# Two-layer graph network, between the layers: GpSimd waits for its own gathers every eight, VectorE scales x1 from the fourth block on

## The chip, the cores and the metric

The kernel runs on one core of a Trainium2 chip. The metric is the device time of the whole program in microseconds (us). Three executions of the kernel before gave 2437.67, 2437.79 and 2443.56 us, a median of 2437.79. A further execution was taken with the hardware profiler: 2439.11 us, of which 2437.4 us lie between the first and the last instruction (the span).

## The reference

There are 6250 nodes with 128 features and 100000 edges, sorted by their target node. Layer 0 computes a message for each edge, takes the maximum over the edges of each target, adds it to the node's features and normalizes each row. Layer 1 sums the weighted rows of the sources into each target, multiplies by a weight matrix, adds a bias and the residual, and normalizes again.

```python
h = x @ W1 + b1
e = concatenate([h[dst], h[src] - h[dst]], axis=-1)
m = relu(relu(e @ W2 + b2) @ W3 + b3)
x = layernorm(x + relu(segment_max(m, dst, num_segments=6250)))      # layer 0, then x1
AX = segment_sum(edge_weight[:, None] * x[src], dst)
x = layernorm(x + (AX @ W.T + b))                                    # layer 1
```

## The kernel before, in words

The nodes are held as 49 columns of 128 rows, one node per partition. The program has four stages: preparation of tables (to about 118 us of the span), the edge loop of layer 0 (to about 1360 us), the stretch between the layers (1360 to 1468 us), and layer 1 (the rest: a loop over 196 groups of edges, then a loop that sums 409 pairs of tiles). Each engine has an instruction list written out by hand; the order in it is the order of issue, and the lists meet only at semaphores. The change touches the stretch between the layers alone.

What each engine does there, with its lines in the kernel before:

- GpSimd (POOL) gathers the maxima. The edge loop left running maxima in the table `seg_tab` in memory; for each of the 49 node columns one indirect DMA (line 455) brings the 128 rows at the ends of the nodes' segments into `rows`. The 49 columns form seven blocks of 8, 8, 8, 8, 8, 6 and 3 columns (`NORM`, semaphores `seg_ld`, each with its own). The dictionary `beats` lets GpSimd wait before columns 24, 28, 32, 36, 40, 44 and 46 until VectorE has reached a given block.
- VectorE (DVE), after it has built small tables and one-hot matrices (line 929), adds the gathered rows to `x` for a block (line 1173), takes the moments (lines 1109 and 1112), and after ScalarE's square root makes the reciprocal and the shift (lines 1119 and 1120, semaphore `rstd_done`).
- ScalarE (ACT) takes the square root of a block (line 729), scales and shifts it into `x1` (line 735, one instruction for each column, semaphore `x1_done`), and copies finished products to their compact places (`place`, line 673). A place copy goes to an offset that is read from memory into registers first (line 666), and each of the 49 copies waits for the one before. Places of a block follow two blocks behind its scaling (`BEHIND = 2`).
- TensorE (PE) compacts: for each batch of four columns it multiplies `x1` by the one-hot matrices (line 1377), into one of four PSUM banks. When all 49 columns are placed it multiplies the compact nodes by the layer's weights (line 1521, 13 batches, `xw`). ScalarE copies the even batches out of PSUM (line 746), VectorE the odd ones (line 1225).
- SyncE (SP) issues 50 stores of zeros of 200 KB each (line 562) into the table of layer 1, behind them four loads of `row_bc` (line 516) that VectorE needs for its first `pick` matrices (line 1187), then four more, then the stores of `xw` (line 577) and the loads of layer 1's windows of rows (line 572). They stand in one list, so that none can overtake the zeros.

In VectorE's list the four first picks and four small tables (line 1194) stand ahead of its first copy of `xw`. They wait for all blocks of `x1` and for SyncE's loads of `row_bc`.

Of the kernel before, what the change touches and what calls it, by code (L numbers as in the profile page):

```python
# [12 lines left out]
GT = 4  # L13
# [5 lines left out]
G = T // GT  # L19
UN = 4  # L20
IT = G // UN
RING = 3 * UN
RB = 6
AHEAD = 4
LATE = 2
BEHIND = 2
BEAT = 5
# [6 lines left out]
NORM = [8, 8, 8, 8, 8, 6, 3]  # L34
NC = len(NORM)
# [30 lines left out]
NB = -(-H // GT)  # L66
# [7 lines left out]
ALU = mybir.AluOpType  # L74
# [8 lines left out]
def gnn_kernel(nc, x, src, dst, edge_weight, W1, b1, W2, b2, W3, b3, WL, bL, out):  # L83
    ds = bass.ds
    IOA = bass.IndirectOffsetOnAxis
    with ExitStack() as ctx:
# [6 lines left out]
        def sem(name):  # L93
            return ctx.enter_context(nc.semaphore(name))

        def dram(name, shape, dt=F32):
# [59 lines left out]
        chunk_of = [c for c in range(NC) for _ in range(NORM[c])]  # L156
# [175 lines left out]
        x1_sum, var_done, std_done, rstd_done, x1_done = map(  # L332
            sem, ("x1_sum", "var_done", "std_done", "rstd_done", "x1_done"))
        res_done = sem("res_done")
        rel_ready, perm_step, perm_ready, vals_ps, vals_in = map(sem, ("rel_ready", "perm_step", "perm_ready", "vals_ps", "vals_in"))
# [39 lines left out]
        def batch(b):  # L375

            return range(b * GT, min(H, (b + 1) * GT))
# [7 lines left out]
        def _(pool):  # L385
# [64 lines left out]
            pool.wait_ge(vals_ps, G)  # L450
            beats = {24: (rstd_done, 2), 28: (x1_sum, 3), 32: (rstd_done, 3), 36: (x1_sum, 4), 40: (rstd_done, 4), 44: (x1_sum, 5), 46: (rstd_done, 5)}
            for h in range(H):
                if h in beats:
                    pool.wait_ge(*beats[h])
                pool.indirect_dma_start(rows[:, h, :], None, seg_tab[:, :],
                                        IOA(ap=end_i[:, h:h + 1], axis=0)).then_inc(seg_ld[chunk_of[h]], 16)

# [171 lines left out]
        def _(act):  # L629
# [100 lines left out]

            for c, cols in enumerate(norm_cols):
                roots(0, c)
                act.wait_ge(rstd_done, c + 1)
                for h in range(cols.start, cols.stop):
                    last = nc.scalar.activation(x1[:, h, :], x1_sums[:, h, :], ACT.Identity, bias=shift_by[:, h:h + 1], scale=rstd[:, h:h + 1])
                last.then_inc(x1_done, 1)
                for b in range(NB):
                    if chunk_of[batch(b)[-1]] + BEHIND == c:
                        place(1, b)
            for b in range(NB):  # L740
                if chunk_of[batch(b)[-1]] + BEHIND >= NC:
                    place(1, b)

# [65 lines left out]
        def _(dve):  # L809
# [305 lines left out]
            def scales(n, c):  # L1115

                cols = norm_cols[c]
                dve.wait_ge(std_done, n * NC + c + 1)
                link(V.reciprocal(rstd[:, cols], std[:, cols]))
                V.scalar_tensor_tensor(shift_by[:, cols], mv[:, cols, 0], -1.0, rstd[:, cols], ALU.mult, ALU.mult).then_inc(rstd_done, 1)  # L1120
# [49 lines left out]
            for c, cols in enumerate(norm_cols):  # L1170
                dve.wait_ge(seg_ld[c], 16 * NORM[c])
                for h in range(cols.start, cols.stop):
                    last = V.scalar_tensor_tensor(x1_sums[:, h, :], rows[:, h, :], full[:, h:h + 1], x_sb[:, h, :], ALU.mult, ALU.add)
                last.then_inc(x1_sum, 1)
                dve.wait_ge(x1_sum, c + 1)
                moments(c, x1_sums[:, cols, :])
                scales(0, c)


# [35 lines left out]

            dve.wait_ge(x1_done, NC)
            for r in range(UN):
# [70 lines left out]
        def _(pe):  # L1288
# [223 lines left out]
            for b in range(NB):  # L1512
                pe.wait_ge(x1_done, chunk_of[batch(b)[-1]] + 1)
                place(1, b)
# [86 lines left out]
```

## Time and profile before

| | us |
|---|---|
| median of three runs | 2437.79 |
| profiled execution | 2439.11 |
| its span | 2437.4 |
| TensorE busy | 1886.7 (77% of the span) |
| VectorE busy | 1538.1 (63%) |
| GpSimd busy | 1274.0 (52%) |
| ScalarE busy | 1004.5 (41%) |

The span divides into the stages above. In the page's picture of 40 slices TensorE shows 7 tenths through layer 0, a dip to 2 and 4 tenths in the two slices from 1341 to 1462 us, and 9 tenths through layer 1's loop. The stretch that the change touches lies in that dip. A row of a timeline gives the start, the duration, the engine, the line, the operation, the number of instructions merged into the row, and in brackets the idle time before it with what ended it.

### The profile page before, as it was taken

What the parts mean: (1) busy time and instruction counts of PE and PEld (TensorE: products, weight loads), DVE (VectorE), ACT (ScalarE), POOL (GpSimd) and SP (SyncE); (2) the same over time, 40 slices, a digit from 0 to 9 for tenths busy, and PEclk for the clock granted to TensorE, in tenths of its full rate; (3) what the DMA queues carried; (4) which work ended last, traced back from release to release, by engine and by line L of the source; (5) the groups of instructions that cost most, each with busy time, mean ns of one, the idle gap of its engine ahead of it and who ended that gap; (6) DMA issues with size and microseconds to landing.
All of it is one profiled execution on the core that took longest, in us unless ns stands there. A gap on an engine that the chain in (4) does not pass through costs nothing.

```text
span 2437.4 us, 59448 instructions
## 1 busy us (share of the span) xinstructions
PE 1886.7 (77%) x15384; PEld 1643.7 (67%) x15384; DVE 1538.1 (63%) x4339; ACT 1004.5 (41%) x3045; POOL 1274.0 (52%) x1300
## 2 busy tenths in 40 slices
PE   5657777777777777777777349989999999699994
PEld 5645555555555555555555248888888888699994
DVE  5556666666676766666666844544444444388886
ACT  3413233333233333323333155555555555466666
POOL 6366566666666666666665344666666666400000
PEclk8779899999999999999999669999999999899997
DMA  4445555555555555555555257777777777699995
GB/s 131 123 123 147 148 152 151 152 155 154 154 151 153 155 152 152 151 150 149 146 149 146 89 191 223 231 240 233 238 241 234 239 239 240 214 282 291 286 290 174
DMA packets 533245, 452.12 MB, mean 185 GB/s; under 512 B 59035, under 2 KB 498295, under 8 KB 533152
## 3 DMA queue, kind: packets, MB, share of 16 engines
q1 hardware_dynamic: 374544, 260.16, 37.2%
q0 software_dynamic: 53312, 138.17, 18.3%
q10 hardware_dynamic: 105296, 52.84, 7.4%
q14 instruction: 70, 0.57, 0.1%
q8 instruction: 23, 0.38, 0.1%
HBM read 291.57 MB, written 159.37 MB: 185 GB/s over the span
## 4 chain that ended last, share of the span: by engine, by line
PE 40%; DVE 21%; issue 14%; another core or an unknown queue 14%; DVEq 3%; DMA 3%; ACT 3%; SPq 1%; POOL 0%; ACTq 0%; POOLq 0%
PE z_ps L1542 8%; PE t_ps L1542 7%; PE m_ps L1542 7%; DVE run L1058 7%; DVE whole L1036 4%; DVE oh L957 2%; PE z_ps L1568 2%; PE m_ps L1568 2%; PE z_ps L1467 2%; DMA whole<-tab 2%; PE t_ps L1568 2%; PE t_ps L1476 2%; PE m_ps L1454 2%; PE m_ps L1455 1%
## 5 line engine op out<-in xcount | busy, mean ns | idle before, releaser
L445 POOL DMA_INDIRECT whole<-q_tab,src_ti x784 | 763.0, 973 | 484.9 <-remote 259.8
L468 POOL DMA_INDIRECT tab<-whole,row_at x392 | 405.9, 1036 | 271.9 <-issue 83.2
L1187 DVE TENSOR_SCALAR whole<-row_bc,node_id 128x768 f32<-128x768 uint8 x392 | 229.4, 627 | 332.3 <-DMA row_bc<-rel_tab 281.5
L690 ACT ACTIVATE m<-m_ps,bias 128x512 f32<-128x512 f32 x196 | 134.7, 687 | 677.7 <-remote 641.7
L1454 PE MATMUL m_ps<-ident,whole 128*128 128x128 f32 x1568 | 322.3, 288 | 34.4 <-issue 21.3
L1455 PE MATMUL m_ps<-oh,win 128*128 128x128 f32 x1568 | 314.6, 284 | 1.3 <-issue 1.3
L1454 PEld LDWEIGHTS m_ps<-ident,whole 128*128 128x128 f32 x1568 | 257.0, 205 | 70.4 <-issue 69.8
L985 DVE TENSOR_TENSOR scratch<-s_ps,blk_oh 128x196 f32<-128x196 f32 x196 | 70.6, 360 | 318.5 <-remote 314.2
L1455 PEld LDWEIGHTS m_ps<-oh,win 128*128 128x128 f32 x1568 | 250.9, 201 | 1.9 <-issue 1.9
L1058 DVE TENSOR_TENSOR_SCAN run<-row_bc,run,z_ps 128x512 f32<-128x512 uint8 x195 | 248.2, 1273 | 0.4 <-ACT z_ps L695 0.3
L1476 PEld LDWEIGHTS t_ps<-ident,run 128*128 128x128 f32 x784 | 111.4, 153 | 188.2 <-issue 177.6
L1467 PE MATMUL z_ps<-m,w 128*128 128x512 f32 x392 | 234.7, 683 | 0.0
L1249 DVE TENSOR_TENSOR whole<-iota_f,whole 128x256 f32<-128x256 f32 (+1 forms) x409 | 184.4, 451 | 60.4 <-PE z_ps L1568 32.1
L1476 PE MATMUL t_ps<-ident,run 128*128 128x128 f32 x784 | 157.8, 297 | 71.9 <-issue 69.1
L1542 PE MATMUL t_ps<-win,whole 128*128 128x128 f32 x1560 | 194.6, 279 | 18.9 <-issue 14.5
L1542 PE MATMUL z_ps<-win,whole 128*128 128x128 f32 x1584 | 197.3, 279 | 12.3 <-issue 11.8
L1414 PE MATMUL s_ps<-whole 128*128 128x18 bf16 x784 | 48.4, 171 | 201.0 <-issue 166.2
L1542 PE MATMUL m_ps<-win,whole 128*128 128x128 f32 x1560 | 194.2, 279 | 11.7 <-issue 11.3
L1542 PEld LDWEIGHTS t_ps<-win,whole 128*128 128x128 f32 x1560 | 181.1, 192 | 19.6 <-issue 15.3
L1542 PEld LDWEIGHTS z_ps<-win,whole 128*128 128x128 f32 x1584 | 183.5, 192 | 13.8 <-issue 13.1
L1414 PEld LDWEIGHTS s_ps<-whole 128*128 128x128 bf16 x784 | 36.4, 96 | 230.5 <-issue 228.9
L1542 PEld LDWEIGHTS m_ps<-win,whole 128*128 128x128 f32 x1560 | 180.7, 192 | 13.6 <-issue 13.0
(294 smaller groups left out, 3592.3 us busy)
## 6 DMA issues: line engine op xcount, KB each, us to landing
whole<-tab SPq DMA_DIRECT2D x409, 194.0 KB
win<-p_tab SPq DMA_DIRECT2D x784, 64.0 KB
seg_tab<-run_e ACTq DMA_DIRECT2D x196, 256.0 KB
win<-xw_tab SPq DMA_DIRECT2D x392, 128.0 KB
row_bc<-seg_row_tab SPq DMA_DIRECT2D x196, 128.0 KB
row_bc<-rel_tab SPq DMA_DIRECT2D x196, 96.0 KB
tab<-zeros SPq DMA_DIRECT2D x67, 200.0 KB
whole<-q_tab,src_ti POOLq DMA_INDIRECT x784
```

Of the source, the lines that this page charges most:

```text
L445: pool.indirect_dma_start(qg[:, g % RING, j, :], None, q_tab[:, :], IOA(ap=src_ti[:, t:t + 1], axis=0)).then_inc(q_ld[g % RING], 16)
L468: pool.indirect_dma_start(tab[:, :], IOA(ap=row_at[0:FR, k:k + 1], axis=0), fat[0:FR, k % RR, :], None).then_inc(fat_st[k // GK % RS], 16)
L690: nc.scalar.activation(m1[:, s, :], m1_ps[:, s, :], ACT.Relu, bias=bias12[:]).then_inc(relu1, 1)
L1058: V.tensor_tensor_scan(run[:, s, :], row_bc[:, r % RB, GE:2 * GE], z_ps[:, s, :], first, ALU.mult, ALU.max).then_inc(run_done, 1)
L1187: last = V.tensor_scalar(pick[:, s, j, :], row_bc[:, s, 0:GK * SLOTS], node_id[:, j:j + 1], None, ALU.is_equal)
L1249: V.tensor_tensor(node_hot[:, r % PS, 0:n, :], iota_f[:, :].unsqueeze(1).to_broadcast([P, n, P]), loaded[:, r % PL, 0:n * KW].rearrange("p ...
L1454: mm(m1_ps[:, s, c], lhsT=qg[:, r % RING, j, :], rhs=ident[:], start=True, stop=False)
L1455: last = mm(m1_ps[:, s, c], lhsT=win[:, r % UN, j, :], rhs=oh[:, s, c], start=False, stop=True)
L1467: mm(z_ps[:, s, :], lhsT=w3[:], rhs=m1[:, s, :], start=True, stop=True).then_inc(z_done, 1)
L1476: last = nc.tensor.transpose(t_ps[:, s, c], run[:, s, c], ident[:])
L1542: last = mm(fat_bank[r % 3][0:FR, c, q * P:(q + 1) * P], lhsT=pick[:, r % UN, j, (c * SL + q) * FR:(c * SL + q + 1) * FR], rhs=win[:, r % ...
L1568: last = mm(sum_bank[r % PS], lhsT=node_hot[:, r % PS, q, :], rhs=loaded[:, r % PL, q * KW:q * KW + D], start=q == 0, stop=q == SL - 1)
```

## The change

Four things are changed.

1. GpSimd's `beats` go. In their place it waits before columns 8, 16, 24, 32, 40 and 46 until the gather of the column two before (6, 14, 22, 30, 38, 44) has landed. These six gathers count on semaphores of their own (reused ones of the edge loop); VectorE waits for them beside its block's.
2. In blocks 3 to 6 (25 columns) VectorE makes `x1` itself with one `tensor_scalar` for each column, right behind the block's scales. Blocks 0 to 2 stay with ScalarE.
3. ScalarE's list is written in another order: three blocks scaled, then the places of block 0, the root of block 3, the places of block 1, the root of block 4, the places of blocks 2 and 3, the root of block 5, the places of block 4, the root of block 6, the places of blocks 5 and 6.
4. TensorE and VectorE wait for `x1_done` (blocks 0 to 2) or `x1_late` (blocks 3 to 6).

```diff
-BEHIND = 2
+EARLY = 3
+RESTS = [8, 16, 24, 32, 40, 46]
+FLY = 2
...
+        rest_ld = dict(zip([h - FLY for h in RESTS], q_ld))
+        landed = {h: 16 * (GT * len(range(k, G, RING)) + 1) for k, h in enumerate(rest_ld)}
...
-            beats = {24: (rstd_done, 2), 28: (x1_sum, 3), 32: (rstd_done, 3), 36: (x1_sum, 4), 40: (rstd_done, 4), 44: (x1_sum, 5), 46: (rstd_done, 5)}
             for h in range(H):
-                if h in beats:
-                    pool.wait_ge(*beats[h])
+                if h in RESTS:
+                    pool.wait_ge(rest_ld[h - FLY], landed[h - FLY])
                 pool.indirect_dma_start(rows[:, h, :], None, seg_tab[:, :],
...
-            for c, cols in enumerate(norm_cols):
+            for c, cols in enumerate(norm_cols[:EARLY]):
                 roots(0, c)
                 act.wait_ge(rstd_done, c + 1)
                 for h in range(cols.start, cols.stop):
                     last = nc.scalar.activation(x1[:, h, :], x1_sums[:, h, :], ACT.Identity, bias=shift_by[:, h:h + 1], scale=rstd[:, h:h + 1])
                 last.then_inc(x1_done, 1)
...
+            places_of(0)
+            roots(0, 3)
+            places_of(1)
+            roots(0, 4)
+            places_of(2)
+            places_of(3)
+            roots(0, 5)
+            places_of(4)
+            roots(0, 6)
+            places_of(5)
+            places_of(6)
...
                 scales(0, c)
+                if c >= EARLY:
+                    dve.wait_ge(rstd_done, c + 1)
+                    for h in range(cols.start, cols.stop):
+                        last = V.tensor_scalar(x1[:, h, :], x1_sums[:, h, :], rstd[:, h:h + 1], shift_by[:, h:h + 1], ALU.mult, ALU.add)
+                    last.then_inc(x1_late, 1)
...
-            dve.wait_ge(x1_done, NC)
+            dve.wait_ge(x1_done, EARLY)
+            dve.wait_ge(x1_late, NC - EARLY)
```

ScalarE's list before, from the last place copy of block 0 over block 3's root and scaling to block 1's first places:

```order
L673 ACTIVATE whole<-m_ps 128x128
L729 ACTIVATE std<-mv,eps 128x8
L735 ACTIVATE whole<-whole,shift_by,rstd 128x128 x8
L666 TENSOR_LOAD col_off_i
L673 ISA
L673 ACTIVATE whole<-z_ps 128x128
```

The same place in ScalarE's list of the changed kernel (its line numbers are its own):

```order
L677 ACTIVATE whole<-m_ps 128x128
L733 ACTIVATE std<-mv,eps 128x8
L670 TENSOR_LOAD col_off_i
L677 ISA
L677 ACTIVATE whole<-z_ps 128x128
```

The eight scaling instructions of the block are gone from between the root and the places.

VectorE's list before, from block 3's sums to block 4's (`whole` holds `rows`, `x1_sums` and `x1`):

```order
L1173 SCALAR_TENSOR_TENSOR whole<-whole,full 128x128 x8
L1109 BN_STATS part<-whole 128x6 x8
L1112 BN_AGGR mv<-part 128x2 x8
L1119 RECIPROCAL rstd<-std 128x8
L1120 SCALAR_TENSOR_TENSOR shift_by<-mv,rstd 128x8
L1173 SCALAR_TENSOR_TENSOR whole<-whole,full 128x128 x8
```

The same place in the changed kernel:

```order
L1190 SCALAR_TENSOR_TENSOR whole<-whole,full 128x128 x8
L1123 BN_STATS part<-whole 128x6 x8
L1126 BN_AGGR mv<-part 128x2 x8
L1133 RECIPROCAL rstd<-std 128x8
L1134 SCALAR_TENSOR_TENSOR shift_by<-mv,rstd 128x8
L1198 TENSOR_SCALAR whole<-whole,rstd,shift_by 128x128 x8
L1190 SCALAR_TENSOR_TENSOR whole<-whole,full 128x128 x8
```

The scaling now stands on VectorE between a block's scales and the next block's sums. GpSimd's and SyncE's lists hold the same DMAs in the same order; only GpSimd's waits differ.

## Rows read from the trace of the kernel before

**Rows 1.** GpSimd's timeline: start, duration, engine, line, operation, count, idle before

```profile
1372.80 1.45 POOL L455 DMA_INDIRECT whole<-seg_tab,end_i  x1 [0.30 <-issue]
...
1391.67 0.94 POOL L455 DMA_INDIRECT whole<-seg_tab,end_i  x1 [0.30 <-issue]
1401.76 1.07 POOL L455 DMA_INDIRECT whole<-seg_tab,end_i  x1 [9.14 <-DVE shift_by L1120]
...
1410.68 0.94 POOL L455 DMA_INDIRECT whole<-seg_tab,end_i  x1 [0.30 <-issue]
...
1420.72 0.94 POOL L455 DMA_INDIRECT whole<-seg_tab,end_i  x1 [0.30 <-issue]
1425.57 1.07 POOL L455 DMA_INDIRECT whole<-seg_tab,end_i  x1 [3.91 <-DVE shift_by L1120]
...
1436.01 1.11 POOL L455 DMA_INDIRECT whole<-seg_tab,end_i  x1 [0.30 <-issue]
```

**Rows 2.** SyncE's timeline, 1384 to 1466 us, the zeros by stretch

```profile
1384.31 9.73 SPq L562 DMA_DIRECT2D tab<-zeros  x5
1395.45 8.65 SPq L562 DMA_DIRECT2D tab<-zeros  x12
1403.81 17.20 SPq L562 DMA_DIRECT2D tab<-zeros  x9
1423.81 6.81 SPq L562 DMA_DIRECT2D tab<-zeros  x8
1431.38 4.35 SPq L562 DMA_DIRECT2D tab<-zeros  x3
1437.86 9.85 SPq L562 DMA_DIRECT2D tab<-zeros  x14
1447.76 8.22 SPq L516 DMA_DIRECT2D row_bc<-rel_tab  x8
...
1465.15 0.99 SPq L572 DMA_DIRECT2D win<-xw_tab  x2
```

**Rows 3.** VectorE's timeline, 1360 to 1458 us

```profile
1360.51 3.22 DVE L929 TENSOR_SCALAR win<-iota_f,in_col 128x128 f32<-128x128 f32 x16
...
1373.36 0.77 DVE L1149 CAST whole<-slot_vals 128x1176 int32<-128x1176 f32 x1
...
1386.37 1.64 DVE L1109 BATCH_NORM_STATS2 part<-whole 128x6 f32<-128x128 f32 x8
1392.66 0.88 DVE L1112 BATCH_NORM_AGGREGATE mv<-part 128x2 f32<-128x6 f32 x8 [4.65 <-remote]
...
1413.66 2.19 DVE L1173 SCALAR_TENSOR_TENSOR whole<-whole,full 128x128 f32<-128x128 f32 x8 [6.95 <-DMA whole<-seg_tab,end_i]
...
1417.56 0.64 DVE L1112 BATCH_NORM_AGGREGATE mv<-part 128x2 f32<-128x6 f32 x8
...
1451.31 4.32 DVE L1187 TENSOR_SCALAR whole<-row_bc,node_id 128x768 f32<-128x768 uint8 x8 [5.57 <-DMA row_bc<-rel_tab]
1455.55 1.42 DVE L1194 TENSOR_TENSOR junk<-iota_f,whole 114x256 bf16<-114x256 f32 x4
1457.78 0.69 DVE L1225 COPY whole<-m_ps 128x512 f32<-128x512 f32 x1 [0.81 <-PE m_ps L1521]
```

**Rows 4.** ScalarE's timeline, 1395 to 1454 us

```profile
1395.52 0.30 ACT L729 ACTIVATE std<-mv,eps 128x8 f32<-128x8 f32 x1 [35.75 <-remote]
...
1406.75 3.18 ACT L735 ACTIVATE whole<-whole,shift_by,rstd 128x128 f32<-128x128 f32 x8 [0.47 <-issue]
...
1424.56 0.30 ACT L729 ACTIVATE std<-mv,eps 128x8 f32<-128x8 f32 x1 [11.33 <-remote]
...
1453.88 0.28 ACT L673 ACTIVATE whole<-m_ps 128x128 f32 x1 [0.22 <-ACT whole L673]
```

**Rows 5.** TensorE's timeline: first product of line 1521, first of layer 1's loop

```profile
1454.21 3.53 PE L1521 MATMUL m_ps<-wT,whole 128*128 128x128 f32 x16 [4.62 <-ACT whole L673]
...
1468.42 2.92 PE L1542 MATMUL z_ps<-win,whole 128*128 128x128 f32 x24
```

More of the change, by code:

```diff
@@ L333, in gnn_kernel @@
             sem, ("x1_sum", "var_done", "std_done", "rstd_done", "x1_done"))
+        x1_late = sem("x1_late")
+        rest_ld = dict(zip([h - FLY for h in RESTS], q_ld))
+        landed = {h: 16 * (GT * len(range(k, G, RING)) + 1) for k, h in enumerate(rest_ld)}
         res_done = sem("res_done")
@@ L450, in _ @@
             pool.wait_ge(vals_ps, G)
-            beats = {24: (rstd_done, 2), 28: (x1_sum, 3), 32: (rstd_done, 3), 36: (x1_sum, 4), 40: (rstd_done, 4), 44: (x1_sum, 5), 46: (rstd_done, 5)}
             for h in range(H):
-                if h in beats:
-                    pool.wait_ge(*beats[h])
+                if h in RESTS:
+                    pool.wait_ge(rest_ld[h - FLY], landed[h - FLY])
                 pool.indirect_dma_start(rows[:, h, :], None, seg_tab[:, :],
-                                        IOA(ap=end_i[:, h:h + 1], axis=0)).then_inc(seg_ld[chunk_of[h]], 16)
+                                        IOA(ap=end_i[:, h:h + 1], axis=0)).then_inc(rest_ld.get(h, seg_ld[chunk_of[h]]), 16)
             pool.wait_ge(fat_zero, 1)
@@ L729, in roots, with places_of @@
                 nc.scalar.activation(std[:, cols], mv[:, cols, 1], ACT.Sqrt, bias=eps[:]).then_inc(std_done, 1)
-            for c, cols in enumerate(norm_cols):
+            def places_of(c):
+                for b in range(NB):
+                    if chunk_of[batch(b)[-1]] == c:
+                        place(1, b)
+            for c, cols in enumerate(norm_cols[:EARLY]):
                 roots(0, c)
@@ L736, in _ @@
                 last.then_inc(x1_done, 1)
[L737 to L742, printed above, removed]
+            places_of(0)
[9 more added lines that the diff above has]
+            places_of(6)
             for b in range(0, HX // GT, 2):
@@ L1170, in _ @@
             for c, cols in enumerate(norm_cols):
-                dve.wait_ge(seg_ld[c], 16 * NORM[c])
+                dve.wait_ge(seg_ld[c], 16 * (NORM[c] - sum(h in rest_ld for h in range(cols.start, cols.stop))))
+                for h in range(cols.start, cols.stop):
+                    if h in rest_ld:
+                        dve.wait_ge(rest_ld[h], landed[h])
                 for h in range(cols.start, cols.stop):
@@ L1177, in _ @@
                 scales(0, c)
+                if c >= EARLY:
+                    dve.wait_ge(rstd_done, c + 1)
+                    for h in range(cols.start, cols.stop):
+                        last = V.tensor_scalar(x1[:, h, :], x1_sums[:, h, :], rstd[:, h:h + 1], shift_by[:, h:h + 1], ALU.mult, ALU.add)
+                    last.then_inc(x1_late, 1)
             def picks(i, r):
@@ L1512, in _ @@
             for b in range(NB):
-                pe.wait_ge(x1_done, chunk_of[batch(b)[-1]] + 1)
+                c = chunk_of[batch(b)[-1]]
+                if c < EARLY:
+                    pe.wait_ge(x1_done, c + 1)
+                else:
+                    pe.wait_ge(x1_late, c - EARLY + 1)
                 place(1, b)
```

## The prediction

> **What bounds the kernel now.** I read the profile in this order: the page (span 2437.4 us, where TensorE dips), then the timelines of the five engines through the stretch between the layers, and last SyncE's list in short windows. The question is which wait ends last before layer 1's loop starts at 1468.42 [rows 5]. Behind that point TensorE's lists of layer 1 are untouched, so a microsecond at the start is taken as a microsecond at the end.
>
> Two chains meet there. The first is the chain of x1: gathers, sums, moments, root, scale, place. Its last place copy starts at 1453.88 and ends at 1454.16 [rows 4], and TensorE starts the products of line 1521 at 1454.21 [rows 5]. It is long because of two pauses of GpSimd, 9.14 and 3.91 us, both ended by VectorE's scales [rows 1], and two late starts that no instruction explains: VectorE's aggregates at 1392.66 after 4.65 us idle, and ScalarE's root at 1424.56, although the aggregates it waits for started at 1417.56 and took 0.64, so 6.36 us late [rows 3, 4].
>
> The second is SyncE's list. Its 50 zero stores end at 1447.71, the first row_bc load is issued at 1447.76 [rows 2], and VectorE's picks, which need it, start at 1451.31 after 5.57 us of waiting for that DMA [rows 3]. Picks and tables keep VectorE until 1456.97 (1455.55 + 1.42), and only then can it copy an odd batch of xw; it does so at 1457.78 [rows 3]. So the two chains arrive 0.81 us apart. An earlier x1 gives at most little until SyncE's list is earlier too.
>
> The reader is to see one thing more in rows 1 and 2 together. SyncE issues zeros fast when GpSimd pauses and slowly when it gathers: 12 in 8.65 us and 14 in 9.85 (0.70 to 0.72 each), against 9 in 17.20 (1.91 each) and 5 in 9.73 (1.95) while gathers run. The gain is not instant: after GpSimd restarts at 1401.76 SyncE stays fast for about 2 us, after 1425.57 for about 5, and after GpSimd stops at 1392.61 it resumes at 1395.45. The two unexplained late starts lie in the slow stretches too: VectorE resumes at 1392.66, just when GpSimd's 24th gather ends, and ScalarE at 1395.52 and at 1424.56, each 2.9 us after GpSimd stopped (1392.61, 1421.66).
>
> **The change part by part.**
>
> GpSimd's waits. Two pauses of 9.14 and 3.91 us go (13.05, against 0.30 between any two gathers, so 12.45 us above the ordinary gap). Six rests come. The price of one: a gather lands about 2.0 us after its issue ends (the last of block 3 ended at 1411.62, VectorE starts at 1413.66 [rows 1, 3]). The gather before a rest ends 1.25 us after the one waited for, so the rest is 2.0 - 1.25 = 0.75, with 0.2 for the semaphore 0.95, which is 0.65 above the ordinary gap. Bounds: nothing (already landed) to about 2 us (landing slowed by the zeros). Six make 3.9 us. The last gather starts at 1436.01 - 12.45 + 3.9 = 1427.5 and lands at about 1430.5 instead of 1439. Queued behind a rest is only the next gather.
>
> Scaling on VectorE. 25 instructions of 128x128, which the trace does not show. The nearest rows: 3.22 us for 16 tensor_scalars of line 929 (0.20 each) below, 2.19 for 8 of line 1173 (0.27 each) above [rows 3]. I take 0.20, since it is the same operation and shape: 8 cost 1.6 us, all 25 cost 5.0 (at most 6.8). They stand between blocks, where VectorE waited 6.95 us for a gather in block 3 [rows 3]; gathers come 10 us a block and VectorE needs 2.2 + 1.6 + 0.6 + 0.7 + 0.4 + 1.6 = 7.1, so gathers cover it. On ScalarE 25 scalings of 0.40 (3.18 for 8 [rows 4]) go, 10 us.
>
> The new end of the x1 chain, if no start is late: block 6 is summed from 1430.5, VectorE needs 0.9 + 0.7 + 0.3 + 0.7 + 0.4 + 0.6 = 3.6 us for three columns, TensorE and ScalarE then take two batches, some 4 us: 1438. Against 1454.16 that is 16 us earlier. With the 4.65 and 6.36 us of late starts put back it is 1449, still 5 earlier. So this chain stops being the last.
>
> What is late next: SyncE. Its 50 zeros take 63.4 us from 1384.31. Slow stretches hold 5 + 9 + 3 = 17 (one zero is counted in two windows, so 16) in about 36.6 us, 2.3 each with the gaps between; the other 34 take 26 us, 0.7 to 0.75 each [rows 2]. In the changed kernel gathers run from 1361 to 1428.5, so the slow state would last from 1384.3 to about 1429.5, 45 us instead of 36.6: 45 / 2.3 = 19.6 zeros, and 30.4 at 0.70 = 21.3 us, an end at 1450.8, 3.1 later than before. Each of the four rests that fall after 1384 gives some fast time back. If a rest gave 3 us as the two restarts did, 12 us fast hold 16 zeros, 33 us slow hold 14.3, and 19.7 are left for 13.8 us: an end at 1443.3, 4.4 earlier. A rest is shorter than those pauses and one gather is still in flight, so I take half: 1447, 0.7 earlier. Both ends stay in the range.
>
> What an early x1 gives by itself. With places done by 1449 TensorE fills its four banks and one more, and waits for VectorE's first odd copy, now at 1457.0 instead of 1457.78. It has then eight batches left. From a cold clock the first two cost 3.53 for 16 products and the other six 0.9 each [rows 5]: 1457.7 + 3.5 + 5.4 = 1466.6, where the last product before ended at 1467.57. That is 1.0 us. SyncE's window loads at 1465.15 [rows 2] come 1 to 2 us earlier the same way, since its stores find batches ready.
>
> Sum, against the profiled execution: 2439.1 - 0.7 (SyncE) - 1.0 (products) = 2437.4. The profiled execution lies 1.3 us above the median of the runs shown, so the median to expect is 2436.
>
> One rule speaks against the change. The trace first: gathers beside the tensor_scalars of line 929 took 0.94 to 1.04 us, and one beside the casts of 1176 elements took 1.45 [rows 1, 3], 0.5 more. The Trainium skill ("SBUF — State Buffer", section "SBUF: two separate sides") says that VectorE in a mode with two ports locks GpSimd out, so that it cannot write descriptors, for the whole instruction. By the rule the 25 scalings of 0.20 would hold up gathers by up to 5 us; by the row of line 929 they hold up none. The x1 chain has the room either way.
>
> **The rivals.**
>
> A. The rests do all that the long pauses did: no late starts and SyncE mostly fast. For it: SyncE's restart graces are long, and in layer 0's loop GpSimd rests briefly after every four gathers and all engines run. Against it: the late starts ended only with pauses of 9 and 4 us. All 50 zeros at 0.70 would end at 1419, so the x1 chain with its end at 1438 decides, and layer 1 starts up to 16 us earlier: 2423. Half of that, SyncE's end near 1440, gives 2439.1 - 8 - 1 = 2430, or 2429 as a median.
>
> B. Starved engines, slower. VectorE's wait at 1388 and ScalarE's behind it were ended by GpSimd's pause at 1392.61. If a rest of 0.95 us with one gather in flight does not end such a wait, and it lasts until GpSimd is done at 1428.5, then VectorE and ScalarE take blocks 0 to 2 from 1431 on, 5.2 us a block, so to 1446.5, and ScalarE's 49 place copies, 1.67 us a batch of four, follow: 1467. Layer 1 starts 13 us late: 2452. It decides from the point where the late starts sum to over 16 us. A milder form is SyncE's end at 1450.8 alone: 3.1 - 1.0 = 2.1 us slower, 2440.
>
> C. The order does not matter: late starts are tied to something else, and the end is as before, 2438.
>
> **How the numbers follow.** Forecast (within 4 us of 2436, C and the mild form of B with it) 0.62; A 0.21; B in its strong form 0.17. This kernel's measurement tells a change from none at about 0.3%, 7.3 us. A reaches beyond that in nearly all of its weight, B as well: faster 0.20, same 0.63, slower 0.17. The forecast's own range is 2431 to 2441. The range reaches to half of A and half of B: 2427 to 2447.
>
> **What would show it.** Right: GpSimd's gathers of line 459 in the changed kernel end near 1428.5 with six gaps of about 1 us; places end before 1450; VectorE's picks still wait for row_bc, at 1448 to 1454; the first product of layer 1's loop starts at 1465 to 1470. The scaling shows about 0.20 us an instruction. Wrong to the fast side: zeros at 0.7 us through the gathers and picks before 1445. Wrong to the slow side: a gap of over 10 us on VectorE or ScalarE between 1388 and 1430 that ends with GpSimd's last gather. Wrong altogether: a difference that lies outside the stretch, in either loop.

## The result, and the profile after

The changed kernel takes 2449.74 us (median of nine runs, 2447.59 to 2456.72), the kernel before 2438.89 (nine runs beside them, 2436.62 to 2443.56). The ratio is 1.0051, with a 95% interval of 1.0041 to 1.0062: slower, by 10.9 us between the medians, and outside the predicted range of 2427 to 2447. The profiled execution of the changed kernel took 2447.59 us with a span of 2445.9, so it is 8.5 us longer than that of before. It divides like this: the first gather of the stretch starts 1.1 us later (1362.37 against 1361.28), the stretch from there to the first product of layer 1's loop is 5.3 us longer (112.4 against 107.1), and the rest 2.1 us (971.1 against 969.0). The change has its work in the middle part only.

GpSimd's gathers in the changed kernel, to be set beside [rows 1]; the first, the six behind the rests, and the last:

```profile
1362.37 0.94 POOL L459 DMA_INDIRECT whole<-seg_tab,end_i  x1 [23.90 <-DMA seg_tab<-run_e]
...
1373.03 1.00 POOL L459 DMA_INDIRECT whole<-seg_tab,end_i  x1 [0.54 <-DMA whole<-seg_tab,end_i]
...
1385.13 3.04 POOL L459 DMA_INDIRECT whole<-seg_tab,end_i  x1 [0.83 <-DMA whole<-seg_tab,end_i]
...
1398.10 0.94 POOL L459 DMA_INDIRECT whole<-seg_tab,end_i  x1 [1.19 <-DMA whole<-seg_tab,end_i]
...
1408.92 0.94 POOL L459 DMA_INDIRECT whole<-seg_tab,end_i  x1 [0.69 <-DMA whole<-seg_tab,end_i]
...
1419.12 0.94 POOL L459 DMA_INDIRECT whole<-seg_tab,end_i  x1 [0.47 <-DMA whole<-seg_tab,end_i]
...
1427.05 0.94 POOL L459 DMA_INDIRECT whole<-seg_tab,end_i  x1 [0.74 <-DMA whole<-seg_tab,end_i]
...
1429.54 0.94 POOL L459 DMA_INDIRECT whole<-seg_tab,end_i  x1 [0.30 <-issue]
```

GpSimd does what it should, but for one gather of 3.04 us behind the second rest. The rests are 0.47 to 1.19 us, and the last gather ends at 1430.5 instead of 1437.1. VectorE behind it, to be set beside [rows 3]:

```profile
1409.92 2.19 DVE L1190 SCALAR_TENSOR_TENSOR whole<-whole,full 128x128 f32<-128x128 f32 x8 [3.52 <-DMA whole<-seg_tab,end_i]
1413.56 1.64 DVE L1123 BATCH_NORM_STATS2 part<-whole 128x6 f32<-128x128 f32 x8 [1.45 <-DVE whole L1190]
1424.08 0.58 DVE L1126 BATCH_NORM_AGGREGATE mv<-part 128x2 f32<-128x6 f32 x7 [8.88 <-issue]
1425.45 0.18 DVE L1126 BATCH_NORM_AGGREGATE mv<-part 128x2 f32<-128x6 f32 x1 [0.80 <-issue]
1434.22 0.20 DVE L1133 RECIPROCAL rstd<-std 128x8 f32<-128x8 f32 x1 [8.58 <-ACT std L733]
...
1434.66 2.14 DVE L1198 TENSOR_SCALAR whole<-whole,rstd,shift_by 128x128 f32<-128x128 f32 x8
...
1454.10 0.86 DVE L1198 TENSOR_SCALAR whole<-whole,rstd,shift_by 128x128 f32<-128x128 f32 x3
1455.05 4.32 DVE L1209 TENSOR_SCALAR whole<-row_bc,node_id 128x768 f32<-128x768 uint8 x8
1459.29 1.42 DVE L1216 TENSOR_TENSOR junk<-iota_f,whole 114x256 bf16<-114x256 f32 x4
1463.03 0.69 DVE L1248 COPY whole<-m_ps 128x512 f32<-128x512 f32 x1 [2.31 <-PE m_ps L1548]
```

And ScalarE, beside [rows 4]:

```profile
1405.67 0.30 ACT L733 ACTIVATE std<-mv,eps 128x8 f32<-128x8 f32 x1 [6.72 <-remote]
...
1433.88 0.30 ACT L733 ACTIVATE std<-mv,eps 128x8 f32<-128x8 f32 x1 [20.32 <-remote]
...
1458.88 0.28 ACT L677 ACTIVATE whole<-m_ps 128x128 f32 x1 [0.22 <-ACT whole L677]
```

The reader is to see a hole in block 3. VectorE has the data of the block at 1409.92, and ScalarE takes its root at 1433.88, 24 us later; what lies between is 4.6 us of work on VectorE. The statistics start 1.45 us after the sums. The aggregates wait 8.88 us behind their own engine's statistics, and the page says "issue", which means that it sees nothing they waited for. ScalarE then starts 8.3 us after the last of them ended (1425.63), at 1433.88, which is 3.4 us after GpSimd's last gather. Two rests of GpSimd lie in the hole (1419.12 and 1427.05) and end neither wait. VectorE's wait does end while GpSimd still gathers, ScalarE's only after the last gather. So of the lateness 11.1 us (1.45 + 8.88 + 0.80) lie on VectorE with gathers still coming, and 8.3 on ScalarE. From 1434 on VectorE works through blocks 4 to 6 without any such gap (the longest, 1.79 us, is behind place copies in ScalarE's list), but all gathers had been issued by 1430.5, and the picks of line 1209 start at 1455.05 with no wait for row_bc: VectorE itself is now the last.

SyncE's zeros, by stretch, beside [rows 2] (one zero stands in both of the last two stretches):

```profile
1385.33 8.91 SPq L566 DMA_DIRECT2D tab<-zeros  x11
1395.51 7.62 SPq L566 DMA_DIRECT2D tab<-zeros  x7
1404.22 18.42 SPq L566 DMA_DIRECT2D tab<-zeros  x7
...
1433.15 5.18 SPq L566 DMA_DIRECT2D tab<-zeros  x5
1438.00 11.72 SPq L566 DMA_DIRECT2D tab<-zeros  x19
...
1449.77 9.95 SPq L520 DMA_DIRECT2D row_bc<-rel_tab  x8
```

SyncE issues 18 zeros by 1403.1 (0.99 us each) while gathers run, then 9 in the 28.9 us up to 1433.15 (3.2 each), and the last 23 in 16.6 (0.72 each).

TensorE, beside [rows 5], and the granted clock of its first 4 us and of the rest of line 1548 (the columns of the second view: stretch, length, busy time and count of TensorE, its weight loads, VectorE, ScalarE and GpSimd, granted clock, DMA share, GB/s):

```profile
1459.20 3.78 PE L1548 MATMUL m_ps<-wT,whole 128*128 128x128 f32 x16 [1.70 <-ACT whole L677]
...
1474.80 2.92 PE L1569 MATMUL z_ps<-win,whole 128*128 128x128 f32 x24
```

```profile
1459.00:1463.00 4.00, 3.79 (x18) 3.80 (x19) 1.71 (x5) 0.75 (x2) 0.00 (x0) 0.50 0.22 68
1463.00:1474.80 11.80, 11.07 (x91) 10.90 (x90) 4.43 (x9) 3.58 (x6) 0.00 (x0) 0.91 0.66 183
```

The same two stretches of the kernel before:

```profile
1454.00:1458.00 4.00, 3.79 (x20) 3.79 (x21) 3.19 (x9) 0.76 (x2) 0.00 (x0) 0.58 0.34 93
1458.00:1468.40 10.40, 9.67 (x88) 9.51 (x87) 4.21 (x9) 3.58 (x6) 0.00 (x0) 1.00 0.74 205
```

The places end at 1458.88 + 0.28 = 1459.16, 5.0 us later than before, and from TensorE's first product of the layer's weights to layer 1's loop it takes 15.6 us instead of 14.2, since the granted clock is 0.50 and 0.91 there instead of 0.58 and 1.00 (0.50 is TensorE's lower level of 1.2 GHz, 1.00 its upper one of 2.4). Ahead of both stretches the engine had only short bursts of work with idle time between them. In three of the kernels below, with other waits, the same products took 14.3, 15.0 and 15.4 us (the first, the third and the second kernel of the first set).

One number serves in all that follows. From the first sum of a block of eight (line 1190) to ScalarE's root it takes 4.57 us where nothing is late. What goes beyond it is called the lateness of a block. In the kernel before it is 6.8 us in block 0 and 6.3 in block 3; in the changed kernel 2.1 in block 2 and 19.4 in block 3 (1433.88 - 1409.92 - 4.57).

### The profile page after: what moved, and what is told of

It is laid out like the page before. It is cut to its first block and busy times, and to the rows that moved or that the text cites. A ratio compares the mean times of both kernels' runs of the same rounds, so it can differ in the third digit from the quotient of the medians.

```text
span 2445.9 us, 59454 instructions
## 1 busy us (share of the span) xinstructions
PE 1900.9 (78%) x15384; PEld 1657.7 (68%) x15384; DVE 1544.3 (63%) x4364; ACT 998.7 (41%) x3020; POOL 1278.4 (52%) x1300
## 5 line engine op out<-in xcount | busy, mean ns | idle before, releaser
L1477 PE MATMUL m_ps<-ident,whole 128*128 128x128 f32 x1568 | 327.9, 293 | 33.3 <-issue 21.2
L1499 PE MATMUL t_ps<-ident,run 128*128 128x128 f32 x784 | 156.8, 299 | 72.4 <-issue 68.0
L1569 PEld LDWEIGHTS z_ps<-win,whole 128*128 128x128 f32 x1584 | 183.7, 192 | 15.2 <-issue 14.6
```

The costliest lines, as they stand in the source:

```text
L1477: mm(m1_ps[:, s, c], lhsT=qg[:, r % RING, j, :], rhs=ident[:], start=True, stop=False)
L1499: last = nc.tensor.transpose(t_ps[:, s, c], run[:, s, c], ident[:])
L1569: last = mm(fat_bank[r % 3][0:FR, c, q * P:(q + 1) * P], lhsT=pick[:, r % UN, j, (c * SL + q) * FR:(c * SL + q + 1) * FR], rhs=win[:, r % ...
```

## The experiments

The kernels were run in five sets, each beside the kernel before on one chip. The first set met a chip like that of the result (the kernel before takes 2436.24 us there). The other four met chips on which the same kernel takes 2145 to 2150 us. Which chip a set would meet was not known when its expectations were written; those of the second set reckon with the first kind alone. The experiments are told by kernel, and the set is named. "Kind of chip" is only a name for these two speeds: each chip of the five sets was met in one of them only, so it isn't shown that the chip makes the difference and not the hour or what else ran.

**Half the change each (first set).** The first kernel keeps the scaling on VectorE and the new order, and takes the old waits of GpSimd back:

```diff
-        rest_ld = dict(zip([h - FLY for h in RESTS], q_ld))
+        rest_ld = {}
...
+            beats = {24: (rstd_done, 2), 28: (x1_sum, 3), 32: (rstd_done, 3), 36: (x1_sum, 4), 40: (rstd_done, 4), 44: (x1_sum, 5), 46: (rstd_done, 5)}
             for h in range(H):
-                if h in RESTS:
-                    pool.wait_ge(rest_ld[h - FLY], landed[h - FLY])
+                if h in beats:
+                    pool.wait_ge(*beats[h])
```

> The changed kernel with GpSimd's waits of before put back: the scaling on VectorE and ScalarE's new order stay. Theory S (the short rests leave GpSimd's stream unbroken and starve ScalarE and VectorE until it ends; the scaling is harmless): the late starts are back to 4 to 6 us, the places end by 1450, the time is 2434 to 2440, 9 to 15 us below the changed kernel. Theory V (the loss comes from the scaling on VectorE and the order of ScalarE's list): it stays near 2449.

2433.49 us, ratio 0.9990 (0.9982 to 0.9999). GpSimd's pauses are 5.75 and 2.94 us, the lateness is 2.0, 2.1 and 4.4 us in blocks 0, 1 and 3, and layer 1's loop starts at 1461.87:

```profile
1420.82 0.30 ACT L734 ACTIVATE std<-mv,eps 128x8 f32<-128x8 f32 x1 [10.06 <-remote]
...
1447.56 3.63 PE L1549 MATMUL m_ps<-wT,whole 128*128 128x128 f32 x16 [1.70 <-ACT whole L678]
```

The second is the kernel before (`x1` on ScalarE, its order) with the six short rests:

```diff
+RESTS = [8, 16, 24, 32, 40, 46]
+FLY = 2
...
-                if h in beats:
-                    pool.wait_ge(*beats[h])
+                if h in RESTS:
+                    pool.wait_ge(rest_ld[h - FLY], landed[h - FLY])
...
```

> The kernel before with GpSimd's six short rests in place of its seven beats, all else as before. Theory S: as slow as the changed kernel or slower, 2447 to 2456, with ScalarE's root of block 3 starting only 2 to 4 us after GpSimd's last gather. Theory V: 2430 to 2438, since the gathers end 7 us earlier.

2447.08 us, 1.0047 (1.0032 to 1.0061). Lateness 10.0 us in block 2 and 15.2 in block 3; in block 3 it is VectorE that stands, twice. The first of these waits ends while GpSimd gathers, the second 4.1 us after its last gather (which ended at 1430.04):

```profile
1413.61 0.30 ACT L732 ACTIVATE std<-mv,eps 128x8 f32<-128x8 f32 x1 [14.44 <-remote]
...
1427.70 1.71 DVE L1112 BATCH_NORM_STATS2 part<-whole 128x6 f32<-128x128 f32 x8 [9.50 <-remote]
1434.18 0.64 DVE L1115 BATCH_NORM_AGGREGATE mv<-part 128x2 f32<-128x6 f32 x8 [4.78 <-remote]
```

So the whole loss comes with the short rests; the scaling on VectorE, with ScalarE's new order, costs nothing and gives a little (0.1%, hardly clear of the noise).

**One landing more at each rest (first set).** The changed kernel, waiting for the gather just before the rest instead of the one before that:

```diff
-FLY = 2
+FLY = 1
```

> The changed kernel with each rest lasting until the gather just before it has landed, not the last but one. Rests of 2.2 us in place of about 0.8, the gathers end about 8 us later. Theory S, in the form that a drained gather queue ends a late start: no engine is late by more than 10 us, 2436 to 2444. In the form that only a long pause helps: 2449 to 2456. Theory V: 2449.

2432.88 us, 0.9985 (0.9976 to 0.9994): faster than the kernel before, by 3.4 us between the medians. The rests grow to 1.86 to 3.01 us, the last gather starts at 1436.76, and block 3 has no lateness at all (1416.33 - 1411.76 is 4.57):

```profile
1411.76 2.19 DVE L1190 SCALAR_TENSOR_TENSOR whole<-whole,full 128x128 f32<-128x128 f32 x8 [6.35 <-issue]
...
1416.33 0.30 ACT L733 ACTIVATE std<-mv,eps 128x8 f32<-128x8 f32 x1 [4.42 <-DVE mv L1126]
...
1424.73 1.00 POOL L459 DMA_INDIRECT whole<-seg_tab,end_i  x1 [3.01 <-DMA whole<-seg_tab,end_i]
...
1448.91 3.78 PE L1548 MATMUL m_ps<-wT,whole 128*128 128x128 f32 x16 [1.70 <-ACT whole L677]
```

A further 1.05 to 2.5 us of waiting at each of six places took away the 19.4 us of lateness in block 3. What stays is 1.7 us in block 1.

**The zeros out of the way (first set).** The changed kernel with all gathers held back until the zero stores have landed (the six short rests stay):

```diff
             pool.wait_ge(vals_ps, G)
+            pool.wait_ge(zero_st, 16 * (NPAIR - NF + NX))
             for h in range(H):
```

> The changed kernel with GpSimd's gathers held until SyncE's 50 zero stores have landed. The stores should take 0.7 us each with no gather beside them, so 1384 to 1420; the gathers run 1420 to 1485 alone, and the time is 2495 to 2510. If the late starts need the zero stores beside the gathers, none is over 2 us here; if the unbroken stream of gathers alone makes them, ScalarE or VectorE is again late by 5 to 20 us within it.

2508.12 us, 1.0285 (1.0270 to 1.0300), as it must be with the two one behind the other. What it was run for are the starts:

```profile
1385.49 34.48 SPq L567 DMA_DIRECT2D tab<-zeros  x50
...
1444.41 2.19 DVE L1191 SCALAR_TENSOR_TENSOR whole<-whole,full 128x128 f32<-128x128 f32 x8 [5.01 <-DMA whole<-seg_tab,end_i]
...
1453.31 0.57 DVE L1127 BATCH_NORM_AGGREGATE mv<-part 128x2 f32<-128x6 f32 x7 [5.04 <-issue]
1454.68 0.18 DVE L1127 BATCH_NORM_AGGREGATE mv<-part 128x2 f32<-128x6 f32 x1 [0.79 <-issue]
...
1464.51 0.30 ACT L734 ACTIVATE std<-mv,eps 128x8 f32<-128x8 f32 x1 [21.90 <-remote]
```

The gathers run without zeros from 1422.81 to 1485.5, and the lateness is 15.5 us in block 1 and 20.6 in block 2. The zeros aren't needed for it: on this kind of chip GpSimd's stream of gathers is enough. VectorE is undisturbed until 1448.3, when 20 gathers have been issued. Both waits of block 1 end while the gathers run, as the rows show (aggregates at 1453.31, root at 1464.51). The zeros alone take 0.69 us each, as against 1.29 beside the gathers in the changed kernel (64.39 / 50).

**The changed kernel again (third set, another chip).** No edit.

> The changed kernel once more, beside its variants and the kernel before on one chip. Where the kernel before takes about 2437 us (starved chip): 2446 to 2452, 0.4 to 0.6% slower than before, late starts over 10 us. Where it takes about 2146 us (a chip on which no start was late in four variants): 0.2 to 0.4% faster than before, 2138 to 2142, as the run without any wait was.

2147.27 us against 2149.12, 0.9991 (0.9981 to 1.0000). The rests are there (0.58, 0.81, 1.67, 1.58, 1.21 and 2.50 us), but no block has more than 0.03 us of lateness:

```profile
1166.34 39.17 SPq L566 DMA_DIRECT2D tab<-zeros  x50
...
1196.34 0.30 ACT L733 ACTIVATE std<-mv,eps 128x8 f32<-128x8 f32 x1 [3.47 <-DVE mv L1126]
...
1197.12 2.14 DVE L1198 TENSOR_SCALAR whole<-whole,rstd,shift_by 128x128 f32<-128x128 f32 x8
...
1197.32 0.96 POOL L459 DMA_INDIRECT whole<-seg_tab,end_i  x1 [0.30 <-issue]
1198.58 0.98 POOL L459 DMA_INDIRECT whole<-seg_tab,end_i  x1 [0.30 <-issue]
```

So the loss goes with the late starts, which are absent here, and the same instructions without them are no loss. The late starts aren't a matter of this stretch alone. These are the longest waits in layer 0's edge loop, in the kernel before on the first kind of chip (engine, line, what it waited for: us in total, times, longest):

```profile
ACT m L690 <- remote: 614.5, 178, 4.4
DVE scratch L985 <- remote: 294.7, 178, 2.1
POOL whole L445 <- remote: 250.8, 179, 2.4
```

and in the changed kernel, whose loop is the same, on the second kind (on the first kind its list is like that of before: ScalarE's wait is 593.2 us over 173 times, put down to "remote"):

```profile
ACT m L694 <- PE m_ps L1478: 406.4, 179, 5.7
...
PE m_ps L1477 <- DMA whole<-q_tab,src_ti: 151.5, 146, 2.7
```

On the first kind nearly every group of edges has a wait that the profile puts down to nothing on the core ("remote"); on the second kind there is none in the list. These waits stand there although GpSimd rests some 1.4 us after every four gathers of that loop, so short rests don't keep them away there either. How much of each is late start and how much ordinary waiting the list doesn't say. Of the 303 us between the two executions 219 lie ahead of the first gather, 15 in the stretch and 69 in layer 1.

**A probe (third and fourth sets).** The changed kernel with 60 VectorE instructions of one element a partition between the statistics and the aggregates of block 3, where the changed kernel stood for 8.88 us. If something like a supply of instructions is short, a gap should fall between them.

```diff
+                if c == 3 and probe:
+                    for k in range(60):
+                        V.memset(idle[:, k:k + 1], 0.0)
                 link(last)
...
-                moments(c, x1_sums[:, cols, :])
+                moments(c, x1_sums[:, cols, :], True)
```

> The changed kernel with 60 memsets of one element each, without any semaphore wait among them, in VectorE's list between block 3's statistics and the aggregates that wait for them. If the late starts are slow semaphores alone, the 60 follow each other in under 6 us even while the stream of gathers starves the others, and the gap comes after them; if VectorE is short of instructions, the 60 are themselves spread over 10 us or more, in bursts. Where nothing is starved: 60 in under 6 us and no gap.

> The changed kernel with 60 one-element memsets without waits between block 3's statistics and the aggregates on VectorE. Where other engines are starved (before at about 2437): under 6 us for the 60 and the gap behind them if slow semaphores make the late starts; 10 us or more, in bursts, if VectorE is short of instructions. At about 2146: 60 in under 6 us, no gap.

2151.23 and 2149.72 us, one run each, both on the second kind of chip. In the third set's:

```profile
1196.76 1.06 DVE L1127 MEMSET idle<- 128x1 f32 x59
```

No gap, and none to be found where nothing is late. It tells nothing apart.

**No rests (second, third and fourth sets).** The changed kernel without any wait between the gathers:

```diff
-RESTS = [8, 16, 24, 32, 40, 46]
+RESTS = []
...
-        rest_ld = dict(zip([h - FLY for h in RESTS], q_ld))
+        rest_ld = {}
```

> The changed kernel without any wait of GpSimd between its 49 gathers. The changed kernel's rests were 0.47 to 1.19 us. If they do nothing (a wait has to drain the gathers, theory D), this is within 3 us of the changed kernel, 2446 to 2453, with the late starts up to GpSimd's end near 1426. If they give some relief (what counts is the mean pace of the gathers, theory R), the starts are later still, and the time is 2452 to 2462.

> The changed kernel without any wait between the gathers, again. At about 2437 us for the kernel before: theory D (only a drained queue helps) within 3 us of the changed kernel; theory R (mean pace counts) 3 to 12 us slower than it. At about 2146: within 3 us of the changed kernel.

> The changed kernel without any wait between the gathers. At about 2437 us for the kernel before: theory D (only a drained queue helps) 2446 to 2453, within 3 us of the changed kernel there; theory R (mean pace counts) 2452 to 2462. At about 2146: 0.2 to 0.3% faster than before, as twice already.

2139.50 against 2146.22 (0.9973, 0.9960 to 0.9986), 2144.96 against 2149.12 (0.9980, 0.9968 to 0.9991) and 2142.00 against 2145.26 (0.9986, 0.9973 to 0.9998). The late starts that were expected aren't there. With them gone the kernel without waits is a little faster than the kernel before, three times over; against the changed kernel in the third set (0.9991) the intervals overlap. How such a kernel fares on the first kind of chip wasn't measured.

**A slower stream without rests (second to fifth sets).** As above, with a small GpSimd memset behind each gather that it waits for:

```diff
...
+                nc.gpsimd.memset(idle[:], 0.0).then_inc(pace, 1)
+                pool.wait_ge(pace, h + 1)
```

> As the run without waits, with one GpSimd memset of 128x128 on a spare tile behind each gather, waited for, which spreads the gathers to about 1.5 us each; the queue never drains before the end. Theory R (the others fall behind where GpSimd gathers faster than about one in 1.5 us): no start later than 4 us, gathers end near 1436, 2430 to 2440. Theory D: ScalarE and VectorE are late by 10 us or more from the 20th gather on, 2450 to 2460.

> The changed kernel without waits but with a GpSimd memset of 128x128 behind each gather, again. At about 2437 for the kernel before: theory R 2430 to 2440 and no start over 4 us late; theory D 2450 or more, with starts over 10 us late. At about 2146: 2144 to 2150, as before (2146.8).

> The changed kernel without waits but with a GpSimd memset of 128x128 behind each gather. At about 2437 for the kernel before: theory R 2430 to 2440 and no start over 4 us late; theory D 2450 or more with starts over 10 us late. At about 2146: the same as before.

> The changed kernel without waits but with a GpSimd memset of 128x128 behind each gather. At about 2437 for the kernel before: theory R (mean pace counts) 2430 to 2440 and no start over 4 us late; theory D (only a drained queue helps) 2450 or more with starts over 10 us late. At about 2146: the same as before, as twice already.

1.0009 (0.9995 to 1.0023), 0.9999 (0.9988 to 1.0010), 1.0010 (0.9996 to 1.0024) and 1.0002 (0.9990 to 1.0014). It was meant to tell whether the mean pace of the gathers or a drained queue decides. On chips without late starts it can't. The gathers there take 72.8 us from the first to the last start, instead of 64.2 without the memsets, and the gain of the kernel without rests is gone.

**Few full drains (second set).** The changed kernel with three rests, each waiting for the gather just before it:

```diff
-RESTS = [8, 16, 24, 32, 40, 46]
-FLY = 2
+RESTS = [16, 32, 46]
+FLY = 1
```

> The changed kernel with three rests (before columns 16, 32, 46) that last until the gather just before has landed. The first late start of all traces so far came no sooner than 20 gathers into an unbroken stream. Theory D: 16 gathers between drained queues make none over 3 us, the gathers end near 1432, 2428 to 2434. Theory R (mean 1.39 us a gather against 1.50 with six full drains and 1.31 in the changed kernel): late starts of 3 to 10 us, 2436 to 2445.

2143.33 us, 0.9986 (0.9972 to 1.0000), with rests of 1.79, 3.28 and 3.57 us. Again no lateness.

**Full drains with x1 on ScalarE (second and fourth sets).** The kernel before with six such rests. The edit is that of the second kernel of the first set, with this in place of its `FLY = 2`:

```diff
+FLY = 1
```

> The kernel before with six rests that last until the gather just before has landed, in place of its beats; the scaling of x1 stays on ScalarE in its old order. If the scaling on VectorE is worth something once the starts are in time, this is slower than the changed kernel with the same rests (2432.9), by up to 10 us: 2436 to 2443. If ScalarE's scaling was covered by the gathers, it is within 3 us, 2430 to 2436.

> The kernel before with six rests that drain the gathers, x1 scaled by ScalarE as before. At about 2437 for the kernel before: if the scaling on VectorE is worth something once the starts are in time, 3 to 10 us slower than the changed kernel with the same rests (2432.9), so 2436 to 2443; if not, 2430 to 2436. At about 2146 it was 2154.9.

2154.93 us (1.0044, 1.0029 to 1.0060) and 2152.44 us (1.0032, 1.0021 to 1.0043): slower. The last place copy starts 89.4 us after the first gather (1237.99 - 1148.63), in the changed kernel of the third set 81.5 (1225.17 - 1143.68). Of these 7.9 us 3.3 come from the gathers, which take longer with full drains (74.0 us from the first to the last start against 70.7). Behind the last gather's start it is 15.4 us with the scaling on ScalarE and 10.8 with it on VectorE (10.6 in the kernel with three full drains). So where nothing starts late, ScalarE's list is the last, and the scaling on VectorE with the new order is worth some 4.6 us.

**Scaling on VectorE alone, on the second kind (fifth set).** The first kernel again.

> The changed kernel with GpSimd's waits of before put back. At about 2146 us for the kernel before: nothing is late there, so the old beats cost their own length; they wait for VectorE's scales, which come sooner there; 0.0 to 0.3% slower than the changed kernel's ratio of 0.9991, so 0.999 to 1.002. At about 2437: 0.998 to 1.000, as before (0.9990).

2146.79 us, 0.9978 (0.9965 to 0.9992). The old waits of GpSimd cost 2.1 us of idle time in all there (0.69, 0.48 and 0.93), for VectorE is never behind. The same kernel's pauses were 5.75 and 2.94 us on the first kind of chip. So the long pauses were made by the late starts; whether they also ended them, this pair doesn't show.

## Why the prediction was wrong

**GpSimd's waits: right in the end.** The last gather was to start at 1427.5, and with the 1.1 us of the later first gather that is 1428.6; it started at 1429.54. Six rests of 0.95 us idle were taken; they were 0.54, 0.83, 1.19, 0.69, 0.47 and 0.74, 0.74 on average. That is the 0.75 of the prediction without its 0.2 for the semaphore, a term that no run shows. One gather behind a rest took 3.04 us, which nobody foresaw and which made up for it, so that the good agreement of the end is in part luck.

**Scaling on VectorE: its size at the upper bound.** 2.14 us for 8 is 0.27 each, 6.8 us in all (2.14 + 2.14 + 1.63 + 0.86), where 5.0 were taken and 6.8 was the bound. All 25 ran after the last gather, on the chain that ended last, so nothing covered the difference of 1.8 us. The rule of the Trainium skill ("SBUF — State Buffer", section "SBUF: two separate sides"), by which these scalings would hold the gathers up, found no case in the changed kernel's trace, whose scalings run after the last gather. On the other chip they ran beside each other, and the gathers took 0.96 and 0.98 us. On the first kind, in the kernels with the old waits and with full drains, they took 0.94 to 0.97. What the row of line 929 had said holds there, none of the 5 us.

**SyncE: the end right, by luck.** The zeros end at 1449.72, or 1448.6 without the 1.1 us; 1447 was predicted between 1443.3 and 1450.8. The way there was not as predicted: 2.3 us a zero for as long as gathers run was taken, and it was 0.99 for the first 18 and 3.2 for the next 9, so two errors cancelled. (The slow stretches of the kernel before are also 38.1 us and not 36.6, since the fast ones of [rows 2] sum to 25.3; that moves the predicted end by under half a us.) And this chain is no longer the last.

**The chain of x1: the step that failed.** "With the 4.65 and 6.36 us of late starts put back it is 1449, still 5 earlier. So this chain stops being the last." The 1438 without late starts was sound: it stood 10.5 us behind the start of the last gather, and in the changed kernel on the other chip, where nothing is late, it is 11.1 (1225.17 + 0.28 - 1214.36). Put behind 1429.54 that is 1440.6; the places ended at 1459.16, 18.5 us later, against 19.4 of lateness in block 3. What was wrong is the 11 us. They were read off a kernel with pauses of GpSimd of 9.14 and 3.91 us, and were put into a kernel that has no such pause. The lateness isn't an amount that goes with the work; it depends on GpSimd's waits. Blocks of eight were late by 8.6 us in all in the changed kernel with the old waits, by 21.5 with the short rests, and by 1.7 with full drains. In block 3 of the changed kernel VectorE's part, 11.1 us, ended while GpSimd gathered, and what ended it isn't shown. ScalarE's part, 8.3 us, outlasted the gathers: the root starts 3.4 us after the last gather ends, as it had 2.9 us after GpSimd's stops in the kernel before. The rows held the sign: both late starts of the kernel before ended at a stop of GpSimd or just behind it. The prediction named the mechanism (rival B) and its threshold, "from the point where the late starts sum to over 16 us"; they came to 21.5. It gave it 0.17, with a strong form of 2452 that was worked out for a wait that begins in block 0 and lasts to GpSimd's end. In the run the large lateness began only in block 3, and so was less dear. The sign that the prediction named for this side, a gap of over 10 us that ends with GpSimd's last gather, is ScalarE's 20.32 us before 1433.88.

**The products: the wrong sign.** A gain of 1.0 us was expected from earlier places; the products of line 1548 took 1.4 us more, with the clock at 0.50 and 0.91. The kernels of the first set lie between, at 14.3 to 15.4 us, and no experiment asked what moves the clock's rise. Against the prediction's sum of 2437.4 the profiled 2447.6 is 10.2 more: 5.0 for the later start of the products (1459.20 against 1454.21, 1.1 of it from ahead of the stretch), 1.4 in the products, 1.7 for the two gains that didn't come, and 2.1 behind the stretch.

**The rivals.** A (short rests do all that long pauses did) fails on the first kind of chip in both kernels with one gather in flight, and comes true in part with none in flight: the lateness of block 3 is gone then, and the time is 3.4 us below that of the kernel before in its set, where the milder form had 9. One reason given for A, that in layer 0's loop all engines run, was misread: ScalarE alone has 178 waits there that the page puts down to "remote", 614.5 us in all. C is out too, since the lateness moved with GpSimd's waits.

**What is shown and what stays open.** Shown: on this kind of chip the short rests alone make the loss (0.9990 without them, 1.0047 with them alone); the scaling and the order don't; other engines start late beside the gathers without the zeros too; waiting for one landing more at each rest cures it. Shown as well: in the kernels traced on four other chips nothing starts late, and on the one of them where the changed kernel was run it is no loss (0.9991, interval up to 1.0000). Open: whether it is the drained queue or only the slower mean pace that cures (the first to the last gather take 73.7 us with full drains, 72.4 with the old waits, 67.2 in the changed kernel, and the paced kernel that would tell them apart never met a chip of the first kind); what the starved engines lack, semaphore events or instructions (in the changed kernel, with the zeros first and with the short rests alone, seven aggregates run and the eighth comes 0.8 us later though it waits for no semaphore, which may speak for instructions, but is only a hint); and why the chips differ.

## What to carry to other kernels

A pause that looks like waste may be what lets other engines start: before one is shortened, look for starts on the other engines that no instruction explains ("remote" or "issue" behind work that is long done), see when each of them ended, and price the change also with such a wait running on until the engine that issues the DMAs is done, not only with its old length. Here that gives the root of block 3, though VectorE's wait before it ended sooner. Where a stream of indirect DMAs has to rest, let it wait for the last one it issued: one landing more at each rest was worth 0.66% here (1.0051 against 0.9985, in two sets of runs on chips of the first kind). Where nothing starts late it bought nothing: there the kernel without any rest was at 0.9973 and the one with three full drains at 0.9986, with overlapping intervals. And a difference of half a per cent that hangs on such waits should be measured on more than one chip, since it was gone on the next.

## What the hardware showed that was not expected

- The same kernel took 2436 to 2439 us in two sets of runs and 2145 to 2150 in four others, 12% apart. The traces of the first kind have late starts, those of the second have none (the kernel before itself was traced on the first alone).
- On the first kind no late start of a block on VectorE or ScalarE came before 20 gathers had been issued. It was 20 in the kernels with the zeros first and with the old waits and the scaling on VectorE, 21 in the kernel before (1388.0, when VectorE could have taken block 0's aggregates), 22 with full drains, and 28 in both kernels with the short rests. Some late starts end while the gathers run (1405.67 and 1424.08 in the changed kernel); those that outlast the gathers or end in a long pause end 0.05 to 6.4 us after the last one was issued (the longest with the zeros first, 1491.83 against 1485.46).
- A zero store of 200 KB takes SyncE 0.69 us alone, 0.78 beside gathers on the second kind of chip (39.17 / 50), and 1.0 to 1.3 beside them on the first (50.04 and 64.39 for 50). The Trainium skill ("DMA: Bandwidth & Descriptors", section "SWDGE vs HWDGE vs iDMA") says that the two kinds of DMA feed different queues inside a DMA engine, which takes turns between them. By that alone the zeros should slow alike on both kinds of chip; they took 0.78 and 1.3 us in the same kernel, and what makes the difference no run here shows.
- A VectorE tensor_scalar of 128x128 with two scalars a partition took 0.27 us, with one scalar 0.20 [rows 3].
- The first gather behind the second rest took 3.04 us in the changed kernel and 3.06 on the other chip, against 0.94 for its neighbours; no experiment asked why.
